# Cross-channel attention on one core: ten of sixteen batches turned by VectorE instead of eight, and the plain copies of G asked for by ScalarE

## The chip, the cores and the metric

One NeuronCore of a Trainium2 chip runs the kernel; nothing else is on the chip. The metric is the device time of one execution in microseconds, smaller is better. Profiles are taken of one execution by the hardware profiler.

## The reference, cut to what matters

X and G (`x`, `ctx`) are 16 batches of 128 x 1024 f32. With rgb = X^T and geo = G^T per batch, 8 heads of 16 channels:

```
attn(q, k) = softmax(q^T k / 4)   per head, 16 x 16, summed over the 1024 positions
rgb_att = rgb + (v_geo attn(q_rgb, k_geo)) proj_p2r^T
geo_att = geo + (v_rgb attn(q_geo, k_rgb)) proj_r2p^T
out     = rgb_att^T + geo_att^T
```

The kernel folds it: one 128 x 128 Gram matrix per batch (X times G^T over the 1024 positions) gives both score matrices after small products with the weights; the softmaxed scores and the weights give two 128 x 128 matrices T, and out = T0 X + T1 G (the identity for the residual is added into T).

## The kernel before, in words

**The work of a batch.** The Gram product needs X and G with positions on the partitions, so both have to be turned. For batches "on tensor" TensorE turns them: 16 transposes of 128 x 128 (line 262), whose PSUM results ScalarE (X, line 402) and VectorE (G, line 478) copy to `xt` and `gt`. For batches "on vector" (`VECTOR_PAIRS`, line 26) the DMA does the coarse part: a pair of batches is loaded a second time in blocks of 1 KB rows into `xz` and `gz` (`load_turned`, line 149), one DMA of 256 KB for each quad, which is a quarter of the 128 partitions (quad 0 is partitions 0 to 31), eight DMAs for a pair's X and G. VectorE's 32 x 32 block transpose (line 471) finishes it, in halves, two of X and two of G per batch. `xz` and `gz` hold two pairs (PAIRS). Every batch is also loaded plainly (X and G, 512 KB each, `x_raw`, `g_raw`, six slots), since the last product needs it unturned: ScalarE rounds it to a high part (`split_hi`, line 389), GpSimd subtracts for the low part (lines 200, 203), and TensorE makes the output in twelve matmuls of 512 columns (line 303). ScalarE copies the output out of PSUM (line 396) and SyncE stores it (line 215, five slots).

**The order.** Every engine runs a hand-written software pipeline over the iteration number i. In iteration i TensorE does, in this order: the output product of batch i-4, the small uv product of i-2, the transposes of batch i if it is on tensor, the y product of i-3, the Gram product of i-1 in two halves, the t product of i-3 and the scores of i-2. VectorE in iteration i turns batch i if it is on vector: first half of X, then the softmax's reciprocal and probabilities of i-3, then first half of G and second half of X, then the copy of y, then the second half of G. ScalarE in iteration i makes the exponentials, splits X of i-2, evacuates the output of i-4, copies uv, splits G of i-2, and copies t.

**Who asks for what.** SyncE asks for all plain copies except batch 0's G: batches 1 to 4 at the start, batch b from 5 on in iteration b-1 if b is on vector and b-3 if not, after waiting until GpSimd is done with batch b-6 in that slot (lines 230 to 234). It asks for quads 0 and 1 of each turned pair (lines 235 to 241) and for the stores, store i-5 in iteration i, which waits for ScalarE's copy. ScalarE asks for quads 2 (early in its iteration) and 3 (after it has split G). Iterations for the turned loads come from `issued_in`: pair 0 in 2, pair 1 in 4, a later pair one iteration after the second batch of the pair two before it; X in that iteration, G in the next.

Of the kernel before, what the change touches and what calls it, by code (L numbers as in the profile page):

```python
# [15 lines left out]
RAW_SLOTS = 6  # L16
# [6 lines left out]
WQR, WKR, WKP, WQP, PP, PR, WVP, WVR = range(8)  # L23


VECTOR_PAIRS = ((5, 6), (8, 9), (11, 12), (14, 15))


def bass_cross_channel_attention(nc: bass.Bass, x, ctx, weights, out):
# [9 lines left out]
    B, C, N = x.shape  # L39
# [5 lines left out]
    on_vector = [b for pair in VECTOR_PAIRS for b in pair]  # L45
# [3 lines left out]
    with ExitStack() as stack:  # L49
# [13 lines left out]
        x_raw = sb("x_raw", [P, RAW_SLOTS, N])  # L63
        g_raw = sb("g_raw", [P, RAW_SLOTS, N])
# [42 lines left out]
        x_loaded = [sem(f"x_loaded{s}") for s in range(RAW_SLOTS)]  # L107
        g_loaded = [sem(f"g_loaded{s}") for s in range(RAW_SLOTS)]
# [32 lines left out]
        x_lo_ready = sem("x_lo_ready")  # L141
        g_lo_ready = sem("g_lo_ready")
# [19 lines left out]
        def x_turned_half(eng, b, half):  # L162
# [3 lines left out]
            else:  # L166
                eng.wait_ge(xt_copied, 2 * on_tensor.index(b) + 1 + half)


        issued_in = {2 + 2 * pair if pair < PAIRS else VECTOR_PAIRS[pair - PAIRS][1] + 1: pair  # L170
                     for pair in range(len(VECTOR_PAIRS))}

# [32 lines left out]

        @block.sync
        def _(sp):
            def load_plain(b):
                slot = b % RAW_SLOTS
                sp.dma_start(x_raw[:, slot, :], x[b]).then_inc(x_loaded[slot], 16)  # L210
                sp.dma_start(g_raw[:, slot, :], ctx[b]).then_inc(g_loaded[slot], 16)

            def store(b):
                sp.wait_ge(half_copied, 2 * b + 2)
                sp.dma_start(out[b], out_sb[:, b % OUT_SLOTS, :]).then_inc(out_stored[b % OUT_SLOTS], 16)

            sp.dma_start(x_raw[:, 0, first], x[0][:, first]).then_inc(x_first, 16)
            sp.dma_start(x_raw[:, 0, second], x[0][:, second]).then_inc(x_loaded[0], 16)
            load_plain(1)
            sp.dma_start(w_sb[:, WQR:WKR + 1, :], weights[:, WQR:WKR + 1, :]).then_inc(wu_loaded, 16)  # L220
            load_plain(2)
            sp.dma_start(w_sb[:, WKP:, :], weights[:, WKP:, :]).then_inc(w_loaded, 16)
            load_plain(3)
            load_plain(4)

            for i in range(2, B + 4):
                for b in range(5, B):
                    if i == max(2, b - 1 if b in on_vector else b - 3):  # L230
                        if b >= RAW_SLOTS:
                            sp.wait_ge(x_lo_ready, b - RAW_SLOTS + 1)
                            sp.wait_ge(g_lo_ready, b - RAW_SLOTS + 1)
                        load_plain(b)
                x_pair, g_pair = issued_in.get(i), issued_in.get(i - 1)
                if x_pair is not None:
                    if x_pair >= PAIRS:
                        pair_turned(sp, x_pair - PAIRS)
                    load_turned(sp, x_turn, xz, xz_loaded, x_pair, (0, 1))
                if g_pair is not None:  # L240
                    load_turned(sp, g_turn, gz, gz_loaded, g_pair, (0, 1))
                if i >= 5:
                    store(i - 5)
            for half in range(2):
                sp.wait_ge(half_copied, 2 * B - 1 + half)
                cols = slice(half * HALF, (half + 1) * HALF)
                sp.dma_start(out[B - 1][:, cols], out_sb[:, (B - 1) % OUT_SLOTS, cols]).then_inc(last_stored[half], 16)
            for s in range(OUT_SLOTS):
                sp.wait_ge(out_stored[s], 16 * len(range(s, B - 1, OUT_SLOTS)))
            for half in range(2):  # L250
                sp.wait_ge(last_stored[half], 16)
# [128 lines left out]
        @block.scalar  # L380
        def _(act):
            def split_hi(b, raw, loaded, hi, hi_ready):
                plain_loaded(act, b, loaded)
                if b == 0:
                    act.wait_ge(x_first, 16)
                    act.wait_ge(g_first, 16)
                if b >= SPLIT_SLOTS:
                    act.wait_ge(half_done, 2 * (b - SPLIT_SLOTS) + 2)
                nc.scalar.copy(hi[:, b % SPLIT_SLOTS, :], raw[:, b % RAW_SLOTS, :]).then_inc(hi_ready, 1)  # L389

            def evacuate(b, half):
                act.wait_ge(half_done, 2 * b + 1 + half)
                if half == 0 and b >= OUT_SLOTS:
                    act.wait_ge(out_stored[b % OUT_SLOTS], 16 * (b // OUT_SLOTS))
                cols = slice(half * HALF, (half + 1) * HALF)
                nc.scalar.copy(out_sb[:, b % OUT_SLOTS, cols], out_ps[:, cols]).then_inc(half_copied, 1)  # L396

            def copy_xt(b, half):
                act.wait_ge(xt_done, 2 * on_tensor.index(b) + 1 + half)
                if b >= 2:  # L400
                    act.wait_ge(gram_done, b - 1)
                nc.scalar.copy(xt[:, b % 2, half * HALF:(half + 1) * HALF], xt_ps[:, :]).then_inc(xt_copied, 1)  # L402

            nc.scalar.dma_start(g_raw[:, 0, first], ctx[0][:, first]).then_inc(g_first, 16)
            nc.scalar.dma_start(g_raw[:, 0, second], ctx[0][:, second]).then_inc(g_loaded[0], 16)

            for i in range(B + 4):
                s, y, l = i - 2, i - 3, i - 4
                x_pair, g_pair = issued_in.get(i), issued_in.get(i - 1)
                if 0 <= s < B:  # L410
                    act.wait_ge(gram_done, s + 1)
                    if s >= 1:
                        act.wait_ge(uv_done, s)
                    nc.scalar.copy(gram_hi[:, :], gram_ps).then_inc(gram_hi_ready, 1)
                if 0 <= y < B:
                    if y >= 1:
                        act.wait_ge(probs_ready, y)
                    for a in range(2):
                        act.wait_ge(s_masked, 2 * y + 1 + a)
                        nc.scalar.activation(expd[:, a, :], scores[:, a, :], ACT.Exp,  # L420
                                             bias=min_neg[:, a:a + 1], scale=-1.0,
                                             accum_out=row_sum[:, a:a + 1]).then_inc(exp_done, 1)
                if 0 <= s < B:
                    split_hi(s, x_raw, x_loaded, x_hi, x_hi_ready)
                if x_pair is not None:
                    if x_pair >= PAIRS:
                        pair_turned(act, x_pair - PAIRS)
                    load_turned(act, x_turn, xz, xz_loaded, x_pair, (2,))
                if g_pair is not None:
                    load_turned(act, g_turn, gz, gz_loaded, g_pair, (2,))  # L430
                if l >= 0:
                    evacuate(l, 0)
                if l >= 0 and l not in (B - 3, B - 2):
                    evacuate(l, 1)
                if 0 <= s < B:
                    act.wait_ge(uv_done, s + 1)
                    if s >= 1:
                        act.wait_ge(s_done, s)
                    nc.scalar.copy(uv[:, :, :], uv_ps.rearrange("p (a c) -> p a c", a=2)).then_inc(uv_copied, 1)
                if i in on_tensor:  # L440
                    copy_xt(i, 0)
                if 0 <= s < B:
                    split_hi(s, g_raw, g_loaded, g_hi, g_hi_ready)
                if x_pair is not None:
                    load_turned(act, x_turn, xz, xz_loaded, x_pair, (3,))
                if g_pair is not None:
                    load_turned(act, g_turn, gz, gz_loaded, g_pair, (3,))
                if i in on_tensor:
                    copy_xt(i, 1)
                if 0 <= y < B:  # L450
                    act.wait_ge(t_summed, y + 1)
                    if y >= 2:
                        act.wait_ge(half_done, 2 * y - 2)
                    nc.scalar.copy(t_hi[:, y % 2, :, :], t_ps.rearrange("p (a c) -> p a c", a=2)).then_inc(t_hi_ready, 1)  # L454
                if l in (B - 3, B - 2):
                    evacuate(l, 1)
                if i == 1:
                    act.wait_ge(wu_loaded, 16)
                    nc.scalar.copy(wu_hi[:, :, :], w_sb[:, WQR:WKR + 1, :]).then_inc(wu_hi_ready, 1)
# [103 lines left out]
```

## Time and profile before

| | us |
|---|---|
| Median of 3 runs (lowest, highest) | 130.85 (130.83, 130.98) |
| The profiled execution | 130.88 |
| Its span, first to last instruction | 128.8 |
| Busy: TensorE / ScalarE / GpSimd / VectorE | 121.5 / 86.3 / 77.3 / 71.2 |

The span is 2.1 us less than the execution's own time; what lies around it is not in the profile. An engine's busy time is the sum over its instructions, so that the distance to the span is time in which it did nothing. A DMA's time to landing runs from its issue until its semaphore is complete, and includes the time in which it stood behind other DMAs of its queue. The DMA share counts packets in flight and can be a little over 1. The 34.25 MB that the profile counts include the weights.

### The profile page before, as it was taken

To read this page: it belongs to the slowest core of one execution; us is meant where nothing else is said; L and a number is where in the kernel's file an instruction comes from. 1 tells how busy PE (TensorE), PEld (TensorE's weight loads), DVE (VectorE), ACT (ScalarE), POOL (GpSimd) and SP (SyncE) were. 2 spreads that over 40 slices of the span, in tenths; PEclk is the share of its full clock that TensorE was granted. 3 is DMA by queue.
4 is the path that set the end of the run, shared out by engine and by line. 5 is a ranking of instruction groups with operands and counts; after the bars stand their busy time and mean duration, and the time that the engine had idled before them with its cause. 6 is when DMAs were issued, how large, how long until landed. Compare 5 with 4: busy or idle time off the path is not lost.

```text
span 128.8 us, 2675 instructions
## 1 busy us (share of the span) xinstructions
PE 121.5 (94%) x858; PEld 109.8 (85%) x858; DVE 71.2 (55%) x210; ACT 86.3 (67%) x194; POOL 77.3 (60%) x41
## 2 busy tenths in 40 slices
PE   6979999999999999999999999999999999979890
PEld 6859998899999999898989898989989898956560
DVE  0045364537878535969633978762787873433410
ACT  3133967875959595768687686779495959595131
POOL 5000779685586877295958386857649595958000
PEclk9999999999999999999999999999999999999998
DMA  3999999999999999999999999999999240400344
GB/s 102 358 416 408 410 312 258 248 248 270 296 211 275 252 384 353 327 242 350 310 270 397 332 325 245 325 304 283 416 416 380 85 163 0 163 0 23 148 165 163
DMA packets 16349, 34.25 MB, mean 266 GB/s; under 512 B 1360, under 2 KB 9680, under 8 KB 16336
## 3 DMA queue, kind: packets, MB, share of 16 engines
q1 hardware_dynamic: 11696, 29.36, 70.9%
q10 hardware_dynamic: 4640, 4.72, 14.2%
q8 instruction: 7, 0.11, 0.4%
q14 instruction: 6, 0.05, 0.1%
HBM read 25.69 MB, written 8.39 MB: 265 GB/s over the span
## 4 chain that ended last, share of the span: by engine, by line
PE 83%; DMA 5%; ACT 4%; issue 2%; DVE 2%; SPq 1%; ACTq 1%
PE out_ps L303 32%; PE gram_bank L283 21%; PE sy_bank L323 6%; DMA g_raw<-in_ctx_dram 5%; PE gt_ps L262 5%; PE xt_ps L262 4%; PE t_bank L359 3%; PE sy_bank L373 3%; PE t_bank L360 3%; PE sy_bank L372 3%; ACT expd L420 2%; PE uv_bank L314 1%; PE uv_bank L316 1%; PE uv_bank L315 1%; DVE probs L512 1%
## 5 line engine op out<-in xcount | busy, mean ns | idle before, releaser
L200 POOL TENSOR_TENSOR x_lo<-x_raw,x_hi 128x1024 fp32r<-128x1024 f32 x16 | 38.0, 2377 | 38.5 <-ACT x_hi L389 38.5
L203 POOL TENSOR_TENSOR g_lo<-g_raw,g_hi 128x1024 fp32r<-128x1024 f32 x16 | 38.0, 2376 | 2.0 <-ACT g_hi L389 2.0
L283 PE MATMUL gram_bank<-gt,xt 128*128 128x128 f32 x256 | 33.8, 275 | 0.0
L283 PEld LDWEIGHTS gram_bank<-gt,xt 128*128 128x128 f32 x256 | 31.2, 192 | 0.0
L396 ACT COPY out_sb<-out_ps 128x512 f32<-128x512 f32 x32 | 18.6, 581 | 4.5 <-PE out_ps L303 3.1
L478 DVE COPY gt<-gt_ps 128x512 f32<-128x512 f32 x16 | 11.0, 688 | 19.1 <-PE gt_ps L262 19.1
L420 ACT ACTIVATE expd<-scores,min_neg 128x128 f32<-128x128 f32 x32 | 12.6, 395 | 8.6 <-DVE min_neg L491 8.6
L389 ACT CAST g_hi<-g_raw 128x1024 fp32r<-128x1024 f32 x16 | 16.9, 1055 | 0.0
L389 ACT CAST x_hi<-x_raw 128x1024 fp32r<-128x1024 f32 x16 | 16.6, 1035 | 0.0
L402 ACT COPY xt<-xt_ps 128x512 f32<-128x512 f32 x16 | 9.4, 587 | 9.2 <-PE xt_ps L262 9.2
L454 ACT CAST t_hi<-t_bank 128x256 fp32r<-128x256 f32 x16 | 6.0, 372 | 14.1 <-DVE t_bank L529 14.1
L303 PE MATMUL out_ps<-x_hi,t_hi 128*128 128x512 f32 x32 | 14.1, 442 | 0.2 <-ACT t_hi L454 0.2
L303 PE MATMUL out_ps<-g_lo,t_hi 128*128 128x512 f32 x32 | 12.8, 399 | 0.0
L303 PE MATMUL out_ps<-x_lo,t_hi 128*128 128x512 f32 x32 | 12.7, 397 | 0.0
L303 PE MATMUL out_ps<-g_hi,t_lo 128*128 128x512 f32 x32 | 12.6, 395 | 0.0
L303 PE MATMUL out_ps<-g_hi,t_hi 128*128 128x512 f32 x32 | 12.6, 395 | 0.0
L303 PE MATMUL out_ps<-x_hi,t_lo 128*128 128x512 f32 x32 | 12.6, 394 | 0.0
L529 DVE TENSOR_TENSOR t_bank<-t_bank,ident 128x256 f32<-128x256 f32 x16 | 6.9, 433 | 9.8 <-PE t_bank L360 9.8
L524 DVE COPY y_sb<-sy_bank 128x256 f32<-128x256 f32 x16 | 6.8, 425 | 9.9 <-PE sy_bank L323 9.9
L471 DVE STREAM_TRANSPOSE gt<-gz 128x512 f32<-128x512 f32 x16 | 11.2, 702 | 0.0
L323 PE MATMUL sy_bank<-w_sb,probs 128*128 128x128 f32 x64 | 9.9, 277 | 1.2 <-DVE probs L512 1.2
L471 DVE STREAM_TRANSPOSE xt<-xz 128x512 f32<-128x512 f32 x16 | 11.0, 685 | 0.0
(49 smaller groups left out, 206.4 us busy)
## 6 DMA issues: line engine op xcount, KB each, us to landing
x_raw<-in_x_dram SPq DMA_DIRECT2D x15, 512.0 KB, 15.1
g_raw<-in_ctx_dram SPq DMA_DIRECT2D x15, 512.0 KB, 14.6
out_dram<-out_sb SPq DMA_DIRECT2D x15, 512.0 KB, 14.5
xz<-in_x_dram SPq DMA_DIRECT2D x8, 256.0 KB, 12.1
gz<-in_ctx_dram SPq DMA_DIRECT2D x8, 256.0 KB, 14.6
xz<-in_x_dram ACTq DMA_DIRECT2D x8, 256.0 KB, 10.8
gz<-in_ctx_dram ACTq DMA_DIRECT2D x8, 256.0 KB, 13.4
x_raw<-in_x_dram SPq DMA_DIRECT2D x2, 256.0 KB, 4.4
```

Of the source, the lines that this page charges most:

```text
L200: nc.gpsimd.tensor_tensor(x_lo[:, slot, :], x_raw[:, raw_slot, :], x_hi[:, slot, :].bitcast(F32), ALU.subtract).then_inc(x_lo_ready, 1)
L203: nc.gpsimd.tensor_tensor(g_lo[:, slot, :], g_raw[:, raw_slot, :], g_hi[:, slot, :].bitcast(F32), ALU.subtract).then_inc(g_lo_ready, 1)
L262: last = nc.tensor.transpose(ps[:, t * TILE:(t + 1) * TILE], raw[:, b % RAW_SLOTS, cols], ident2[:, 0, :])
L283: last = nc.tensor.matmul(gram_ps, xt[:, b % 2, cols], gt[:, b % 2, cols], start=(t == 0), stop=(t == TILES - 1))
L303: last = nc.tensor.matmul(out_ps[:, cols], w[:, b % 2, which, :], moving[:, slot, cols], start=(n == 0), stop=(n == len(parts) - 1))
L323: last = nc.tensor.matmul(y_ps[:, a * P:(a + 1) * P], probs[:, a, :], w_sb[:, wv, :], start=True, stop=True)
L389: nc.scalar.copy(hi[:, b % SPLIT_SLOTS, :], raw[:, b % RAW_SLOTS, :]).then_inc(hi_ready, 1)
L396: nc.scalar.copy(out_sb[:, b % OUT_SLOTS, cols], out_ps[:, cols]).then_inc(half_copied, 1)
L402: nc.scalar.copy(xt[:, b % 2, half * HALF:(half + 1) * HALF], xt_ps[:, :]).then_inc(xt_copied, 1)
L420: nc.scalar.activation(expd[:, a, :], scores[:, a, :], ACT.Exp, bias=min_neg[:, a:a + 1], scale=-1.0, accum_out=row_sum[:, a:a + 1]).then_ ...
L471: nc.vector.transpose(dst[:, b % 2, cols].rearrange("p (j a k) -> p j a k", a=QUADS, k=QUAD), blocks[:, first:first + TILES // 2, :, :]).t ...
L478: nc.vector.tensor_copy(gt[:, b % 2, half * HALF:(half + 1) * HALF], gt_ps[:, :]).then_inc(gt_ready, 1)
```

## The change

`VECTOR_PAIRS` gets a fifth pair and different members: batches 5 to 8 and 10 to 15 are turned by VectorE; TensorE turns 0 to 4 and 9. So 2.10 MB more are loaded (X and G of two batches in turned blocks), and by the rule of `issued_in` pair 1 is asked for in iterations 4 and 5 (X, G) and used from 7, pair 2 in 7 and 8 and used from 10, pair 3 in 9 and 10 and used from 12, pair 4 in 12 and 13 and used from 14. Before, pair 1 was asked for in 4 and 5 and used from 8, pair 2 in 7 and 8 and used from 11, pair 3 in 10 and 11 and used from 14. G's plain copies of batches 1 to 15 are asked for by ScalarE, behind its split of G in the iteration, with the wait for GpSimd's low part of G of batch b-6; SyncE keeps X's with the wait for the low part of X alone. The quads stay divided as they were.

```diff
--- before.py
+++ after.py
@@ -23,7 +23,7 @@
 WQR, WKR, WKP, WQP, PP, PR, WVP, WVR = range(8)
 
 
-VECTOR_PAIRS = ((5, 6), (8, 9), (11, 12), (14, 15))
+VECTOR_PAIRS = ((5, 6), (7, 8), (10, 11), (12, 13), (14, 15))
 
 
 def bass_cross_channel_attention(nc: bass.Bass, x, ctx, weights, out):
@@ -166,6 +166,11 @@
             else:
                 eng.wait_ge(xt_copied, 2 * on_tensor.index(b) + 1 + half)
 
+        def plain_issued_in(i):
+
+
+            return [b for b in range(5, B) if i == max(2, b - 1 if b in on_vector else b - 3)]
+
 
         issued_in = {2 + 2 * pair if pair < PAIRS else VECTOR_PAIRS[pair - PAIRS][1] + 1: pair
                      for pair in range(len(VECTOR_PAIRS))}
@@ -205,10 +210,10 @@
 
         @block.sync
         def _(sp):
-            def load_plain(b):
-                slot = b % RAW_SLOTS
-                sp.dma_start(x_raw[:, slot, :], x[b]).then_inc(x_loaded[slot], 16)
-                sp.dma_start(g_raw[:, slot, :], ctx[b]).then_inc(g_loaded[slot], 16)
+            def load_plain_x(b):
+                if b >= RAW_SLOTS:
+                    sp.wait_ge(x_lo_ready, b - RAW_SLOTS + 1)
+                sp.dma_start(x_raw[:, b % RAW_SLOTS, :], x[b]).then_inc(x_loaded[b % RAW_SLOTS], 16)
 
             def store(b):
                 sp.wait_ge(half_copied, 2 * b + 2)
@@ -216,22 +221,16 @@
 
             sp.dma_start(x_raw[:, 0, first], x[0][:, first]).then_inc(x_first, 16)
             sp.dma_start(x_raw[:, 0, second], x[0][:, second]).then_inc(x_loaded[0], 16)
-            load_plain(1)
+            load_plain_x(1)
             sp.dma_start(w_sb[:, WQR:WKR + 1, :], weights[:, WQR:WKR + 1, :]).then_inc(wu_loaded, 16)
-            load_plain(2)
+            load_plain_x(2)
             sp.dma_start(w_sb[:, WKP:, :], weights[:, WKP:, :]).then_inc(w_loaded, 16)
-            load_plain(3)
-            load_plain(4)
-
-
+            load_plain_x(3)
+            load_plain_x(4)
 
             for i in range(2, B + 4):
-                for b in range(5, B):
-                    if i == max(2, b - 1 if b in on_vector else b - 3):
-                        if b >= RAW_SLOTS:
-                            sp.wait_ge(x_lo_ready, b - RAW_SLOTS + 1)
-                            sp.wait_ge(g_lo_ready, b - RAW_SLOTS + 1)
-                        load_plain(b)
+                for b in plain_issued_in(i):
+                    load_plain_x(b)
                 x_pair, g_pair = issued_in.get(i), issued_in.get(i - 1)
                 if x_pair is not None:
                     if x_pair >= PAIRS:
@@ -388,6 +387,11 @@
                     act.wait_ge(half_done, 2 * (b - SPLIT_SLOTS) + 2)
                 nc.scalar.copy(hi[:, b % SPLIT_SLOTS, :], raw[:, b % RAW_SLOTS, :]).then_inc(hi_ready, 1)
 
+            def load_plain_g(b):
+                if b >= RAW_SLOTS:
+                    act.wait_ge(g_lo_ready, b - RAW_SLOTS + 1)
+                nc.scalar.dma_start(g_raw[:, b % RAW_SLOTS, :], ctx[b]).then_inc(g_loaded[b % RAW_SLOTS], 16)
+
             def evacuate(b, half):
                 act.wait_ge(half_done, 2 * b + 1 + half)
                 if half == 0 and b >= OUT_SLOTS:
@@ -403,6 +407,8 @@
 
             nc.scalar.dma_start(g_raw[:, 0, first], ctx[0][:, first]).then_inc(g_first, 16)
             nc.scalar.dma_start(g_raw[:, 0, second], ctx[0][:, second]).then_inc(g_loaded[0], 16)
+            for b in range(1, 5):
+                load_plain_g(b)
 
             for i in range(B + 4):
                 s, y, l = i - 2, i - 3, i - 4
@@ -441,6 +447,8 @@
                     copy_xt(i, 0)
                 if 0 <= s < B:
                     split_hi(s, g_raw, g_loaded, g_hi, g_hi_ready)
+                for b in plain_issued_in(i):
+                    load_plain_g(b)
                 if x_pair is not None:
                     load_turned(act, x_turn, xz, xz_loaded, x_pair, (3,))
                 if g_pair is not None:
```

## Rows read from the trace of the kernel before

**Rows 1.** The page: busy time by engine, DMA in 40 slices, the chain by engine.
```profile
PE 121.5 (94%) x858; PEld 109.8 (85%) x858; DVE 71.2 (55%) x210; ACT 86.3 (67%) x194; POOL 77.3 (60%) x41
...
DMA  3999999999999999999999999999999240400344
...
PE 83%; DMA 5%; ACT 4%; issue 2%; DVE 2%; SPq 1%; ACTq 1%
```

**Rows 2.** The chain of waits: start us, us, what; where iterations 10, 11, 12, 14 begin.
```profile
64.24 2.81 PE out_ps L303 x12
67.40 0.44 PE xt_ps L262 x4
...
72.28 2.81 PE out_ps L303 x12
...
78.56 2.81 PE out_ps L303 x12
...
92.87 2.80 PE out_ps L303 x12
```

**Rows 3.** Groups by line: the copies of VectorE and ScalarE, and the two turns.
```profile
L478 DVE COPY gt<-gt_ps 128x512 f32<-128x512 f32 x16 | 11.0, 688 | 19.1 <-PE gt_ps L262 19.1
L402 ACT COPY xt<-xt_ps 128x512 f32<-128x512 f32 x16 | 9.4, 587 | 9.2 <-PE xt_ps L262 9.2
L471 DVE STREAM_TRANSPOSE gt<-gz 128x512 f32<-128x512 f32 x16 | 11.2, 702 | 0.0
L471 DVE STREAM_TRANSPOSE xt<-xz 128x512 f32<-128x512 f32 x16 | 11.0, 685 | 0.0
```

**Rows 4.** GpSimd in order of time: the low part of G, batch 10, in iteration 12.
```profile
83.29 2.37 POOL L203 TENSOR_TENSOR g_lo<-g_raw,g_hi 128x1024 fp32r<-128x1024 f32 x1
```

**Rows 5.** The page, DMA queues: packets, MB, share of 16 engines; q1 is SyncE, q10 ScalarE.
```profile
q1 hardware_dynamic: 11696, 29.36, 70.9%
q10 hardware_dynamic: 4640, 4.72, 14.2%
```

**Rows 6.** Busy time by stretch; the last two columns are DMA share and GB/s.
```profile
4.00:96.00 92.00, 90.71 (x661) 83.28 (x659) 56.66 (x162) 65.54 (x148) 57.36 (x25) 1.00 1.06 319
16.00:91.30 75.30, 75.08 (x540) 69.30 (x539) 48.05 (x142) 56.29 (x129) 53.33 (x24) 1.00 1.06 298
92.00:96.00 4.00, 4.00 (x25) 3.46 (x25) 3.97 (x12) 3.23 (x9) 1.17 (x2) 1.00 1.02 418
...
0.00:91.30 91.30, 89.03 (x658) 82.14 (x659) 52.37 (x150) 63.59 (x140) 57.24 (x33) 1.00 1.03 305
...
16.00:20.00 4.00, 3.95 (x34) 3.59 (x32) 2.49 (x10) 2.84 (x9) 3.08 (x3) 1.00 1.04 319
20.00:22.00 2.00, 1.83 (x17) 1.83 (x18) 0.67 (x2) 1.55 (x3) 2.00 (x2) 1.00 1.13 241
```

**Rows 7.** Line 154, G's last quad of pair 3 from ScalarE: start, time to landing.
```profile
L154 ACTq DMA_DIRECT2D gz<-in_ctx_dram x1: 341/341/341, 75.5 to 75.5; - x1
DMA to landing us min/median/max: 15.8/15.8/15.8
```

**Rows 8.** Line 154, G's eight quads from ScalarE together.
```profile
L154 ACTq DMA_DIRECT2D gz<-in_ctx_dram x8: 317/318/341, 17.8 to 75.5; - x8
DMA to landing us min/median/max: 9.2/13.4/15.8
```

**Rows 9.** VectorE in iteration 14: pair 3, first half of G; the copy of y.
```profile
94.76 0.70 DVE L471 STREAM_TRANSPOSE gt<-gz 128x512 f32<-128x512 f32 x1
...
96.50 0.42 DVE L524 COPY y_sb<-sy_bank 128x256 f32<-128x256 f32 x1 [0.45 <-PE sy_bank L323]
```

**Rows 10.** Line 210, batch 14's plain copy of X: start, time to landing.
```profile
L210 SPq DMA_DIRECT2D x_raw<-in_x_dram x1: 1732/1732/1732, 79.9 to 79.9; - x1
DMA to landing us min/median/max: 15.1/15.1/15.1
```

**Rows 11.** After the last matmul; PEclk is the third column from last.
```profile
126.00:128.80 2.80, 0.00 (x0) 0.00 (x0) 0.00 (x0) 0.33 (x1) 0.00 (x0) 0.83 0.43 161
```

## The prediction

> **What bounds the kernel now.** I read the page first: TensorE is busy 94% of the span and makes 83% of the chain that ended last [rows 1]. The DMA line of the same page stands at 9 from the second slice to the thirtieth: until about 97 us the DMA engines are as full as TensorE is [rows 1]. Two resources are at their limit together, and the change takes work from one and gives work to the other. The chain of waits gives the pace of TensorE: iteration 10, whose batch it turns itself, lasts 72.28 - 64.24 = 8.04 us, iteration 11, whose batch VectorE turns, 78.56 - 72.28 = 6.28 us [rows 2]. The difference, 1.76 us, is four groups of four transposes of 0.44 us each, two of X and two of G; one is shown [rows 2].
>
> Then I read how far ahead the data is. G's last quad of pair 3, which ScalarE asked for at 75.54, took 15.8 us and landed at 91.3 [rows 7]. VectorE used it at 94.76 [rows 9]. So a load that was asked for three iterations ahead is there 3.4 us early, no more. The eight quads of G from ScalarE took 9.2 to 15.8 us, 13.4 in the middle [rows 8]; that is queueing, since each is 0.26 MB.
>
> **The change part by part.** *TensorE* loses the 32 transposes of two batches: 2 x 1.76 = 3.52 us, all on the chain [rows 2]. This is the whole gain: 130.88 - 3.52 = 127.4.
>
> *VectorE and ScalarE.* Per batch that moves, VectorE gives two copies of 0.688 and takes two turns of 0.702 and two of 0.685, +1.40 us, and ScalarE gives two copies of 0.587 [rows 3]. VectorE is busy 55% of the span and ScalarE 67% [rows 1], and batches in `VECTOR_PAIRS` already run this program at 6.28 us. Cost nothing; with the cover gone VectorE's would be 2.8 us.
>
> *The asks.* ScalarE gets 15 plain copies and four quads, at 0.32 us each in its queue [rows 8]: 6 us over the kernel, 11 of the plain ones inside the loop at one or two an iteration, where it idles a third of the time; nothing. SyncE gives 15 and gets four; it has time. *The moved wait.* ScalarE now waits for GpSimd's low part of G of batch b-6, and behind that wait stand quad 3, its second copy of X out of PSUM and the copy of t, for which TensorE waits. Tightest is batch 9, asked for in iteration 6 against batch 3, whose low part is made in iteration 5. In iteration 12 that part ends at 83.29 + 2.37 = 85.66, 7.1 us after the iteration began [rows 2, 4]; ScalarE gets to its ask 3.3 us into the next iteration (75.54 - 72.28 [rows 2, 7]), that is 6.28 + 3.3 = 9.6 us after it, 2.5 us later. Cost nothing while TensorE keeps its pace.
>
> *The DMA work.* 2.10 MB more, all in turned blocks. Their price: from 4 to 96 us the DMA engines were full and moved 319 GB/s x 92 us = 29.3 MB [rows 6]. The stretch from 92 to 96 us has plain rows alone and runs at 418 GB/s [rows 6]. The four turned pairs are 8.39 MB, so that the other 21.0 MB would take 50 us at that rate, and 42 us are left for the turned ones: 5.0 us per MB, **10.5 us per pair**. Bounds: at 418 GB/s, 5.0 us; at the mean of the stretch with turned loads in it, 298 GB/s [rows 6], 7.0 us. Two vector batches then need six plain transfers (3.15 MB, 7.5 us) and one pair, 18.0 us of DMA, against 2 x 6.28 = 12.6 us of TensorE. Before, a tensor batch stood between the pairs: 21.8 us of DMA against 20.6 of TensorE, nearly even, as the full DMA line says. After it, pairs follow each other without one in three places of four.
>
> A row shows that full engines can move little: from 20 to 22 us, when the first turned pair is being loaded, the share is 1.13 and only 241 GB/s move [rows 6]. The Trainium skill (SBUF — State Buffer, section "Door 1: The DMA port swizzle") gives a reason: partitions 0 to 63 reach only 8 of the 16 ports, and it gives 218 GB/s for them; by it alone a pair takes 9.6 us. It also says (DMA: Bandwidth & Descriptors, section "Issuing engines are not separate DMA queues") that asking from two engines saves only the time of asking, which speaks against any gain from the moved asks; no run here has shown it yet.
>
> **When pair 4 lands.** In the kernel before, 305 GB/s x 91.3 us = 27.8 MB had moved when G's last quad of pair 3 landed [rows 6]. X of batch 14 was then still on its way (79.86 + 15.1 = 95.0 us [rows 10]). In the changed kernel G of pair 4, the one used from batch 14, is asked for after all of that and more: one more pair (2.10 MB), X and G of batch 14 (1.05), and about a store and a half that was still queued (0.8), 3.95 MB. At 418 GB/s that is 9.4 us, at 298 GB/s 13.3 us, with the turned price of 10.5 us and the rest at 418 it is 14.9 us. I take 14.1, between the last two, since the added part has more turned bytes in it (53%) than that stretch had (37%). Landing: 91.3 + 14.1 = 105.4 us.
>
> It is wanted 3.52 us earlier than before, at 94.76 - 3.52 = 91.2 us, and about 0.5 us of lateness is free (copy of y at 96.50 waits for TensorE by 0.45 us [rows 9]). So **TensorE stands still for 13.7 us in all**, split over pairs 2, 3 and 4, little at pair 2, most at 3 and 4. Net: 13.7 - 3.5 = +10.2 us. Sum: 130.88 + 10.2 = **141.0 us**. From there to the end all is as before. The profiled execution (130.88) lies 0.03 above the median of the runs (130.85), which changes nothing.
>
> *The clock.* After the last matmul, with TensorE idle, the granted clock averages 0.83, that is it fell from its level of 2.4 GHz towards 1.2 GHz within 2.8 us [rows 11]. A standstill of 5 to 7 us could do the same, and the matmuls after it run slower. Price between 0 and 2 us; I take 0, since a slower TensorE before the last standstill is hidden in it, and keep 2 for the range.
>
> **Rivals.** *B, the data comes in time; faster: 127.4.* Pair 4 must then be there by 91.7: 27.8 + 3.95 = 31.8 MB in 91.7 us, 347 GB/s in place of 305. For it: with the plain copies on both queues the two might be full together more often, and from 16 to 20 us, with both queues in turned blocks, 319 GB/s moved [rows 6]; q1 carried 29.4 MB and q10 only 4.7 [rows 5]. Against it: the engines were already full, whatever queue fed them, and 347 is above every stretch with turned blocks that I read. Below 347 GB/s the gain shrinks by 0.26 us per GB/s, and at about 333 GB/s the change comes out even.
>
> *C, only the last pair is late, because it is asked for late.* ScalarE asks for G's last quad 3.3 us into iteration 13 and VectorE wants it 1.9 us into iteration 14 [rows 2, 9]: 6.28 - 3.3 + 1.9 + 0.5 = 5.4 us for a load that took 9.2 to 15.8 [rows 8]. This costs 3.8 to 10.4 us however well the DMA runs: 127.4 + 3.8 to 10.4 = 131.2 to 137.8. It is the floor under the forecast too, unless the queues run empty. The condition is that the mean rate is good enough for pairs 2 and 3 (about 335 GB/s).
>
> *D, ScalarE is held in its own asks.* If its DMA queue fills, the ask itself lasts longer, and everything behind it on ScalarE with it; that comes on top: 143 to 147. The case that the change does not do what it says is small: the transposes are gone for certain; the asks that are moved may bring nothing, and the sum counts nothing for them.
>
> **How the numbers follow.** Forecast 0.70 (own range 136 to 144.5), B 0.12 (127.4 to 130.6), C 0.12, D 0.06. Faster by over 0.2%, about what a measurement can tell from no change here: 0.11, all from B; within 0.2%: 0.03, between B and C; slower 0.86. The range leaves out most of B and the upper end of D: 132.5 to 145.5.
>
> **What the profile after would show.** Line 262 with 96 transposes in place of 128, VectorE's turns of X and of G 20 each. DMA moved 36.3 MB and the line of nines reaches about 110 us. In the chain, DMA `gz` stands with some 10 us, and VectorE waits at line 471 in iterations 12 and 14, TensorE after it. G's last quad of pair 4 lands near 105. Wrong would be: no idle of VectorE before its turns of G; a rate above 340 GB/s up to 90 us; ScalarE's asks longer than 0.4 us (then D).

## The result, and the profile after

The changed kernel takes 139.9 us (median of four runs, 138.8 to 141.6) against 130.9, a ratio of 1.066 (95% interval 1.059 to 1.073). It is slower by 9.0 us; 141.0 was forecast. The profiled execution took 139.08 us with a span of 136.9, 8.1 us longer than the span before. Medians and ranges here are over all executions of a kernel, and ratios only over those within 1.5% of its fastest; where that is a single one, no ratio is stated.

The page of the changed kernel: busy time by engine, three of the lines in 40 slices, the two DMA queues, the chain by engine, three of the DMA issues (the last number is the median time to landing).

```profile
PE 121.7 (89%) x826; PEld 109.3 (80%) x826; DVE 73.9 (54%) x214; ACT 84.1 (61%) x190; POOL 77.4 (57%) x41
...
PE   7958999999999999999999999996509999979790
PEclk9999999999999999999999999999755799999999
DMA  4999999999999999999999999999994030300434
...
q1 hardware_dynamic: 10624, 22.55, 51.3%
q10 hardware_dynamic: 7888, 13.63, 32.0%
...
PE 59%; DMA 26%; ACT 4%; issue 3%; DVE 3%; SPq 1%; ACTq 1%; DVEq 0%
...
x_raw<-in_x_dram SPq DMA_DIRECT2D x15, 512.0 KB, 16.4
g_raw<-in_ctx_dram ACTq DMA_DIRECT2D x15, 512.0 KB, 9.5
gz<-in_ctx_dram ACTq DMA_DIRECT2D x10, 256.0 KB, 11.6
```

TensorE is as busy as before in microseconds and less in share: 121.7 us in a longer span [rows 1]. It has 32 transposes (3.5 us) less to do, but part of its work now runs at the lower clock (below). The slices show where it stopped: one gap in the digits 6, 5 and 0, about 92 to 103 us, with the granted clock low in it and behind it. The DMA line is full up to there, without a gap. In the chain the DMA has gone from 5% to 26%. ScalarE's queue now moves 13.6 MB, SyncE's 22.6 [rows 5].

The chain of waits of the changed kernel (start us, us, what). Each `out_ps` row is the beginning of an iteration: 4, 5, 8, 9, 10, 13, 15, 16.

```profile
2.59 10.96 DMA x_raw<-in_x_dram
...
24.35 2.79 PE out_ps L302 x12
...
32.38 2.82 PE out_ps L302 x12
...
51.80 2.81 PE out_ps L302 x12
...
58.08 2.81 PE out_ps L302 x12
...
66.11 2.80 PE out_ps L302 x12
...
85.04 2.82 PE out_ps L302 x12
...
88.70 12.62 DMA gz<-in_ctx_dram
...
103.00 0.80 PE t_bank L358 x2
103.80 0.43 PE t_bank L359 x2
104.23 1.71 PE gram_bank L282 x8
...
106.79 3.27 PE out_ps L302 x12
...
111.74 0.22 PE t_bank L358 x2
...
113.53 2.81 PE out_ps L302 x12
```

Four things are to be seen. Iteration 4 begins at 24.35; before, it began at 23.05 (`23.05 2.81 PE out_ps L303 x12` in the chain of the kernel before), and a wait for X's plain copy now stands at the head of the chain. Iterations 5 to 7 last 19.42 us in place of 3 x 6.28 = 18.84. Iterations 10 to 12 run at pace: from 66.11 to 85.04 are 18.93 us, 0.1 too long. Iterations 13 and 14 last from 85.04 to 106.79, 21.75 us in place of 12.56: here 9.2 us are lost. The sum is -3.5 + 1.3 + 0.6 + 0.1 + 9.2, and 0.5 in the output product that begins at 106.79 (3.27 in place of 2.81): +8.2 us, which is the difference of the spans.

VectorE in order of time, its turns that waited for a load (in brackets the idle time before, and what ended it):

```profile
48.08 0.71 DVE L479 STREAM_TRANSPOSE gt<-gz 128x512 f32<-128x512 f32 x1 [1.17 <-DMA gz<-in_ctx_dram]
...
81.32 0.71 DVE L479 STREAM_TRANSPOSE gt<-gz 128x512 f32<-128x512 f32 x1 [0.68 <-DMA gz<-in_ctx_dram]
...
94.78 0.71 DVE L479 STREAM_TRANSPOSE xt<-xz 128x512 f32<-128x512 f32 x1 [2.71 <-DMA xz<-in_x_dram]
...
101.34 0.71 DVE L479 STREAM_TRANSPOSE gt<-gz 128x512 f32<-128x512 f32 x1 [4.97 <-DMA gz<-in_ctx_dram]
```

Pair 1 is late by 1.2 us in iteration 7 and pair 3 by 0.7 in iteration 12, where TensorE loses the 0.1 us. In iteration 14 VectorE waits 2.7 us for the last quad of X and then 5.0 for the last of G. No turn of pair 2 waited.

Busy time by stretch (TensorE's clock and the GB/s are the third from last and the last column):

```profile
0.00:101.30 101.30, 92.83 (x665) 84.73 (x665) 58.39 (x165) 66.09 (x147) 63.23 (x35) 0.98 1.04 322
16.00:91.30 75.30, 74.71 (x530) 68.73 (x531) 51.92 (x149) 55.97 (x128) 54.30 (x24) 1.00 1.07 319
101.00:106.00 5.00, 3.00 (x14) 3.00 (x15) 3.08 (x6) 0.40 (x2) 0.00 (x0) 0.50 0.59 240
108.00:110.00 2.00, 2.00 (x10) 1.61 (x9) 1.94 (x5) 1.52 (x4) 0.82 (x1) 1.00 0.00 0
```

While G's last quad was on its way, 322 GB/s x 101.3 us = 32.6 MB had moved. From 16 to 91.3 us the engines moved 319 GB/s, where the kernel before moved 298 with as full a share [rows 6]. And from 101 to 106 us, at the end of the standstill and after it, the clock is granted at 0.50, the 1.2 GHz level; from 108 us on it is back at 1.00.

### The profile page after: what moved, and what is told of

It reads as the page before. It is cut to its first block, busy times and chain, and to the rows that moved or that the text cites. A ratio compares the mean times of both kernels' runs of the same rounds, so it can differ in the third digit from the quotient of the medians.

```text
span 136.9 us, 2603 instructions
## 1 busy us (share of the span) xinstructions
PE 121.7 (89%) x826; PEld 109.3 (80%) x826; DVE 73.9 (54%) x214; ACT 84.1 (61%) x190; POOL 77.4 (57%) x41
## 4 chain that ended last, share of the span: by engine, by line
PE 59%; DMA 26%; ACT 4%; issue 3%; DVE 3%; SPq 1%; ACTq 1%; DVEq 0%
PE out_ps L302 25%; DMA gz<-in_ctx_dram 18%; PE gram_bank L282 14%; DMA x_raw<-in_x_dram 8%; PE sy_bank L322 4%; PE t_bank L358 3%; PE xt_ps L261 3%; PE sy_bank L372 2%; PE t_bank L359 2%; PE sy_bank L371 2%; PE gt_ps L261 2%; ACT expd L426 2%; DVE xt L479 1%; DVE y_sb L532 1%; PE uv_bank L313 1%
## 5 line engine op out<-in xcount | busy, mean ns | idle before, releaser
L282 PE MATMUL gram_bank<-gt,xt 128*128 128x128 f32 x256 | 35.1, 282 | 0.0
L282 PEld LDWEIGHTS gram_bank<-gt,xt 128*128 128x128 f32 x256 | 32.4, 198 | 0.0
L426 ACT ACTIVATE expd<-scores,min_neg 128x128 f32<-128x128 f32 x32 | 12.6, 395 | 9.0 <-DVE min_neg L499 9.0
L479 DVE STREAM_TRANSPOSE gt<-gz 128x512 f32<-128x512 f32 x20 | 14.1, 702 | 6.8 <-DMA gz<-in_ctx_dram 6.8
L486 DVE COPY gt<-gt_ps 128x512 f32<-128x512 f32 x12 | 8.3, 688 | 16.2 <-PE gt_ps L261 16.2
L479 DVE STREAM_TRANSPOSE xt<-xz 128x512 f32<-128x512 f32 x20 | 13.7, 686 | 2.7 <-DMA xz<-in_x_dram 2.7
L302 PE MATMUL out_ps<-g_hi,t_lo 128*128 128x512 f32 x32 | 12.6, 395 | 0.0
L302 PE MATMUL out_ps<-x_hi,t_lo 128*128 128x512 f32 x32 | 12.6, 394 | 0.0
L358 PE MATMUL t_bank<-w_sb,y_sb 128*128 128x128 f32 x32 | 7.0, 301 | 5.3 <-DVE y_sb L532 5.3
L322 PEld LDWEIGHTS sy_bank<-w_sb,probs 128*128 128x128 f32 x64 | 8.4, 190 | 4.0 <-issue 4.0
```

The lines of the kernel that those rows point to most:

```text
L282: last = nc.tensor.matmul(gram_ps, xt[:, b % 2, cols], gt[:, b % 2, cols], start=(t == 0), stop=(t == TILES - 1))
L302: last = nc.tensor.matmul(out_ps[:, cols], w[:, b % 2, which, :], moving[:, slot, cols], start=(n == 0), stop=(n == len(parts) - 1))
L322: last = nc.tensor.matmul(y_ps[:, a * P:(a + 1) * P], probs[:, a, :], w_sb[:, wv, :], start=True, stop=True)
L358: nc.tensor.matmul(t_ps[:, 0:P], y_sb[:, 1, :], w_sb[:, PR, :], start=True, stop=True)
L479: nc.vector.transpose(dst[:, b % 2, cols].rearrange("p (j a k) -> p j a k", a=QUADS, k=QUAD), blocks[:, first:first + TILES // 2, :, :]).t ...
L486: nc.vector.tensor_copy(gt[:, b % 2, half * HALF:(half + 1) * HALF], gt_ps[:, :]).then_inc(gt_ready, 1)
```

## The experiments

Two theories were put against each other. S: the DMA engines cannot move the bytes in time, wherever the asks stand. A: the last pair is late because it is asked for late, two iterations before its use, into a queue that is 9 to 18 us long.

**Each half of the change alone.** The first run takes the kernel before and only its table of pairs:

```diff
-VECTOR_PAIRS = ((5, 6), (8, 9), (11, 12), (14, 15))
+VECTOR_PAIRS = ((5, 6), (7, 8), (10, 11), (12, 13), (14, 15))
```

> The kernel before with the five pairs of the change, all plain copies still asked for by SyncE. Theory A (the last pair is late because it is asked for late, two iterations before its use, and its queue is 9 to 13 us long): G's last quad is asked for at the same place, so the standstill of some 7 us in iteration 14 stays and the time is 137 to 140 us. Theory S (the DMA engines cannot deliver; what the forecast held): pairs 2 and 3 are late too, the rate between 16 and 91 us stays near 298 GB/s, and the time is 140 to 143 us. If the moved asks raise the rate (319 GB/s in the changed kernel), this run is slower than the changed kernel; if they do nothing it is equal, less the 1.3 us by which the changed kernel starts later.

The second takes the changed kernel with the four pairs of before:

```diff
-VECTOR_PAIRS = ((5, 6), (7, 8), (10, 11), (12, 13), (14, 15))
+VECTOR_PAIRS = ((5, 6), (8, 9), (11, 12), (14, 15))
```

> The changed kernel with the four pairs of before: the moved asks alone. Both theories: no standstill in the loop, since the pairs are asked for three iterations ahead. The start is 1.3 us later as in the changed kernel, because X of batch 2 lands at 13.6 in place of 10.7 us, so 131.5 to 132.5 us. If the moved asks raise the DMA rate, the line of nines ends before 97 us and pair 3 lands earlier than 91.3 us.

The pairs alone: 140.5 us (136.0 to 142.2). The asks alone: 132.0 us (131.6 to 132.3), ratio 1.008 (1.006 to 1.011). VectorE of the first, all its turns that waited:

```profile
79.53 0.71 DVE L471 STREAM_TRANSPOSE gt<-gz 128x512 f32<-128x512 f32 x1 [0.91 <-DMA gz<-in_ctx_dram]
...
92.88 0.71 DVE L471 STREAM_TRANSPOSE xt<-xz 128x512 f32<-128x512 f32 x1 [2.60 <-DMA xz<-in_x_dram]
...
101.36 0.71 DVE L471 STREAM_TRANSPOSE gt<-gz 128x512 f32<-128x512 f32 x1 [6.78 <-DMA gz<-in_ctx_dram]
```

The chain of waits of the second, its head and iteration 4:

```profile
2.58 10.83 DMA x_raw<-in_x_dram
...
24.21 2.81 PE out_ps L302 x12
```

Busy time by stretch of the second:

```profile
16.00:91.30 75.30, 75.07 (x538) 69.30 (x539) 47.71 (x141) 56.79 (x129) 52.77 (x24) 1.00 1.06 315
```

The pairs make the loss, and at the same place: G's last quad is used at 101.36, in the changed kernel at 101.34. The time does not part the theories here (140.5 lies at the edge of both), the place does: pair 2 never waits and pair 3 only 0.9 us, where theory S had both late. The moved asks alone cost 1.0 us; iteration 4 begins at 24.21, 1.2 us late.

Whether the moved asks raise the rate is open. With five pairs, 316 GB/s moved from 16 to 91.3 us without them and 319 with them. With four pairs it was 298 without them (the kernel before [rows 6]) and 315 with them, though pair 3 landed no earlier for it: its last quad of G was asked for at 77.1 and took 14.6 us, to 91.7, against 91.3. The Trainium skill says (DMA: Bandwidth & Descriptors, section "Issuing engines are not separate DMA queues") that asking from several engines saves only the time of asking. The two kernels with five pairs agree with that, the two with four do not; each rate is from one execution.

**The ask of the last pair, and the bytes before it.** In the changed kernel, ScalarE's four quads of pair 4 together, early in iteration 12:

```diff
-                    load_turned(act, x_turn, xz, xz_loaded, x_pair, (2,))
-                if g_pair is not None:
+                    load_turned(act, x_turn, xz, xz_loaded, x_pair, (2, 3) if x_pair == LAST else (2,))
+                    if x_pair == LAST:
+                        load_turned(act, g_turn, gz, gz_loaded, x_pair, (2, 3))
+                if g_pair is not None and g_pair != LAST:
...
-                if x_pair is not None:
+                if x_pair is not None and x_pair != LAST:
                     load_turned(act, x_turn, xz, xz_loaded, x_pair, (3,))
-                if g_pair is not None:
+                if g_pair is not None and g_pair != LAST:
                     load_turned(act, g_turn, gz, gz_loaded, g_pair, (3,))
```

> The changed kernel, but ScalarE asks for its four quads of pair 4 (X and G, quads 2 and 3) together early in iteration 12, as soon as the buffers are free, in place of over iterations 12 and 13. Theory A: G's last quad is asked for 9 us earlier and lands 4 to 6 us earlier (its queue is still some 12 us long and the four quads follow one another), at 95 to 97 us; the standstill shrinks to 3 to 5 us: 133 to 136 us. Theory S (bytes alone): it only overtakes the plain copies of G of batches 13 and 14, 1.05 MB or 2.5 to 3 us: 136 to 137 us.

(`LAST` is 4, the last pair.) And in the changed kernel, less to move with the asks where they were. The second halves of the plain copies of batches 10 to 15 are not loaded, so part of the outputs of these batches is not computed from their inputs. The same edit is made for G on ScalarE's side:

```diff
-                sp.dma_start(x_raw[:, b % RAW_SLOTS, :], x[b]).then_inc(x_loaded[b % RAW_SLOTS], 16)
+                n = HALF if b >= 10 else N
+                sp.dma_start(x_raw[:, b % RAW_SLOTS, 0:n], x[b][:, 0:n]).then_inc(x_loaded[b % RAW_SLOTS], 16)
```

> The changed kernel with the plain copies of batches 10 to 15 loading only the first 512 of 1024 columns (the second halves of those slots keep older data, so that part of the outputs of these batches is not computed from its inputs). Asks stand where they stood; 2.6 MB less are ahead of pair 4. Theory S: pair 4 lands 6 to 8 us earlier and the standstill nearly goes: 129.5 to 132 us. Theory A (a late ask alone): an ask at 88.7 us is wanted at 93.8; even in shorter queues a quad needs 8.4 us or more, so 3 to 4 us of standstill stay: 132 to 135 us.

The early ask: 133.0 us (132.5 to 134.9), ratio 1.015 (1.011 to 1.019). The lighter load: 133.4 us (131.1 to 134.6). The profiled execution of the early ask was its slowest (134.9), that of the lighter load its fastest (131.1). VectorE of the early ask:

```profile
49.16 0.71 DVE L482 STREAM_TRANSPOSE gt<-gz 128x512 f32<-128x512 f32 x1 [2.47 <-DMA gz<-in_ctx_dram]
...
83.01 0.71 DVE L482 STREAM_TRANSPOSE gt<-gz 128x512 f32<-128x512 f32 x1 [1.29 <-DMA gz<-in_ctx_dram]
...
97.89 0.71 DVE L482 STREAM_TRANSPOSE gt<-gz 128x512 f32<-128x512 f32 x1 [2.90 <-DMA gz<-in_ctx_dram]
```

VectorE of the lighter load:

```profile
92.26 0.71 DVE L481 STREAM_TRANSPOSE xt<-xz 128x512 f32<-128x512 f32 x1 [0.78 <-DMA xz<-in_x_dram]
...
95.69 0.71 DVE L481 STREAM_TRANSPOSE gt<-gz 128x512 f32<-128x512 f32 x1 [2.21 <-DMA gz<-in_ctx_dram]
```

The last quad of G in the chain of waits (when it was asked for, and how long it took), in the early ask and in the lighter load:

```profile
82.06 15.80 DMA gz<-in_ctx_dram
...
88.11 7.55 DMA gz<-in_ctx_dram
```

In the changed kernel it was asked for at 88.70 and took 12.62. The early ask, 6.6 us earlier, brings the landing forward by 3.5 us; three waits of 2.5, 1.3 and 2.9 us are left. With less to move the ask stands where it stood and takes 5.1 us less, and 0.8 + 2.2 us of waits are left in iteration 14 (the 8.4 us that the expectation put under every quad did not hold). So both the place of the ask and the bytes before it decide when the quad lands.

The early ask moves no byte less and takes back 6.9 us of the 9.0 by the medians, where theory S allowed 2.5 to 3. Not all of this is the landing: the clock, which both theories left out, fell less (0.987 over the profiled execution in place of 0.963, and 1.00 in two of the four runs), and the landing itself moved by little more than theory S allowed. So this run speaks against S in its pure form and does not settle it. Nor does the lighter load: its 133.4 us lies in theory A's range (132 to 135) and above S's (129.5 to 132), but its fastest execution in S's. The runs with a third buffer settle it.

**The same early ask, with SyncE asking for all plain copies** (the edit of the early ask, made to the pairs-alone kernel):

> The five pairs, two buffers, plain copies asked for by SyncE as before, and ScalarE asks for its four quads of pair 4 together early in iteration 12. Against the run with the early ask and the moved plain copies (132.5 to 133.4 us) it shows what the moved asks are worth: both theories say the later start of 1.3 us goes away, 131 to 132.5 us. If the moved asks help the last pair (ScalarE's own queue is shorter for its quads here, so they need not), it is slower than 133 us.

It missed: 138.1 us (137.0 to 141.9), ratio 1.051 (1.043 to 1.059), slower than with the moved asks where 131 to 132.5 was expected. Line 155 (`load_turned`) of this kernel, G's two quads of pair 4 from SyncE, then from ScalarE (shortest, middle and longest time of the ask itself in ns, first and last start, and time to landing); then SyncE's ask that stood before its two.

```profile
L155 SPq DMA_DIRECT2D gz<-in_ctx_dram x2: 1537/1850/2164, 83.7 to 85.3; - x2
DMA to landing us min/median/max: 15.3/15.9/16.6
...
L155 ACTq DMA_DIRECT2D gz<-in_ctx_dram x2: 515/516/516, 78.2 to 78.8; - x2
DMA to landing us min/median/max: 14.0/14.7/15.4
...
78.92 4.78 SPq L212 DMA_DIRECT2D g_raw<-in_ctx_dram  x1
```

The same two quads of SyncE in the early-ask kernel with the moved asks:

```profile
L155 SPq DMA_DIRECT2D gz<-in_ctx_dram x2: 432/480/529, 80.1 to 80.5; - x2
DMA to landing us min/median/max: 12.9/13.1/13.3
```

ScalarE's quads are there by 78.8 + 15.4 = 94.2. Now SyncE's are last: it reaches them at 83.7 and 85.3, since the ask before them, G's plain copy of batch 14, alone held it for 4.8 us; they land at 101.9. With the moved asks they are asked for at 80.1 and 80.5 and are there by 93.8. So the moved asks do have a worth here, of some 5 us, which both theories had missed; it is hidden in the change itself, where ScalarE's last quad is later than either. (The two runs were made on two chips, on both of which the kernel before measures 131.0, so the size is not certain.)

**A third buffer for the turned pairs**, so that pair 4 need not wait until pair 2 is turned. First with SyncE asking for all plain copies:

```diff
-PAIRS = 2
+PAIRS = 3
...
-        issued_in = {2 + 2 * pair if pair < PAIRS else VECTOR_PAIRS[pair - PAIRS][1] + 1: pair
-                     for pair in range(len(VECTOR_PAIRS))}
+        issued_in = {2: 0, 4: 1, 7: 2, 9: 3, 10: 4}
```

> The five pairs with the plain copies asked for by SyncE as before, and a third buffer for the turned pairs, so that pair 4 is asked for in iterations 10 (X) and 11 (G) in place of 12 and 13; nothing else moves. Theory A (late ask of the last pair): pair 4 lands before iteration 14, no standstill there, and the 3.5 us of transposes come through but for what pairs 1 and 3 and the plain copies behind it lose: 127.5 to 130 us. Theory S (bytes): the same bytes are due by the same time, and what is gained at pair 4 is lost at pair 3 or at the plain copies of batches 12 to 14 that it has overtaken: 133 us or more.

With `11: 4` in place of `10: 4`:

> As the run with the third buffer, but pair 4 is asked for in iterations 11 and 12. Theory A: the ask of G's last quad stands at 5.4 + 6.3 = 11.7 us before its use, and the queue is 9 to 15 us long, so 0 to 3 us of standstill are left: 128.5 to 132 us. Theory S: as with iterations 10 and 11, 133 us or more.

138.5 us (134.2 to 142.3) and 133.0 us (131.9 to 137.2; ratio 1.011, 1.007 to 1.016). The profiled execution of the first can't be set beside the others, since it ran with a lower clock throughout (below). The second, 132.95 us, lies between the two theories (A 128.5 to 132, S 133 or more). So the same was tried in the changed kernel with its own asks; then with the start as before; then with pair 4 in 11; and the start alone with two buffers. The edit of the start, of which one of four added lines is shown; G of batches 2, 3 and 4 likewise stands behind X of its batch:

```diff
             load_plain_x(1)
+            sp.dma_start(g_raw[:, 1, :], ctx[1]).then_inc(g_loaded[1], 16)
...
-            for b in range(1, 5):
-                load_plain_g(b)
```

> The changed kernel with its own asks, and the third buffer for the turned pairs, pair 4 asked for in iterations 10 and 11. Theory A (each ask too late for a queue of 9 to 18 us, whichever queue it is): all quads of pair 4 land before iteration 14, no standstill, and only the later start of 1.3 us is left against 127.4: 128.5 to 130 us. Theory S (bytes): 132 us or more, with the standstill moved to pair 3 or to the plain copies.

> As the run before it, with the plain copies of G of batches 1 to 4 asked for by SyncE in the order of the kernel before. X of batch 2 then lands near 10.7 in place of 13.6 us and the start is not late: theory A 127.3 to 129 us. Theory S: 1.3 us less than the run before it, still above 131 us.

> As the run before it, with pair 4 asked for in iterations 11 and 12: theory A leaves 0 to 2 us of standstill at pair 4 and takes less from pair 3: 127.5 to 131 us; theory S as there.

> The changed kernel with two buffers, and only the start as in the kernel before (SyncE asks for G of batches 1 to 4). If the late start is due to these asks, iteration 4 begins at 23.0 in place of 24.3 us. The standstill at pair 4 is set by the asks in iterations 12 and 13, which move with TensorE: the time falls by 0.5 to 1.5 us to 137.5 to 139.5. If the bytes set the landing of pair 4, the start does not matter and the time stays at that of the changed kernel.

| third buffer | start as before | pair 4 asked for in | us (range) | ratio (interval) |
|---|---|---|---|---|
| yes | no | 10, 11 | 136.4 (135.0 to 139.6) | 1.034 (1.030 to 1.038) |
| yes | yes | 10, 11 | 135.0 (134.0 to 135.7) | 1.030 (1.025 to 1.036) |
| yes | yes | 11, 12 | 129.8 (128.5 to 132.0) | 0.988 (0.983 to 0.994) |
| no | yes | 12, 13 | 139.4 (136.9 to 142.3) | not stated |

VectorE with pair 4 in 10 and 11, start as before; this is pair 3, in iteration 12:

```profile
85.02 0.71 DVE L480 STREAM_TRANSPOSE gt<-gz 128x512 f32<-128x512 f32 x1 [5.83 <-DMA gz<-in_ctx_dram]
```

VectorE with pair 4 in 11 and 12:

```profile
47.60 0.71 DVE L480 STREAM_TRANSPOSE gt<-gz 128x512 f32<-128x512 f32 x1 [1.85 <-DMA gz<-in_ctx_dram]
...
93.94 0.71 DVE L480 STREAM_TRANSPOSE gt<-gz 128x512 f32<-128x512 f32 x1 [1.22 <-DMA gz<-in_ctx_dram]
```

With pair 4 asked for two iterations earlier its own turns no longer wait, and pair 3, whose quads of G stand among those of pair 4's X, waits 5.8 us. This is what theory S had said of it, the standstill moved to pair 3, and theory A's 128.5 to 130 and 127.3 to 129 us were wrong (136.4 and 135.0 measured). One iteration earlier is right for both: 1.9 us of wait at pair 1 and 1.2 at pair 4 are left and TensorE's clock stays at its higher level for all of the span. Here theory A's range held and theory S's, above 131 us, did not. The second and third rows of the table move the same bytes on the same chip and differ only in when pair 4 is asked for: 135.0 and 129.8 us. With pair 4 in 12 and 13, the fourth row, it is 139.4. No theory that counts bytes alone gives these three. (The expectation of the last experiment puts the 1.9 us in iteration 14; they are those of pair 1.)

This version is 1.1 us faster than the kernel before (129.8 against 130.9, on the same chip), the only one measured that is; the interval leaves out 1, but one of its four runs, 132.0, was slower than the kernel before. Against the same asks in the kernel with SyncE's plain copies (133.0 us, on another chip) it shows again what the moved asks are worth: there SyncE asked for its last quad of G of pair 4 at 81.6 us and it took 18.0, here at 71.6 and 16.2.

The start alone: iteration 4 began again at 23.0 (the chain of waits of the last row of the table):

```profile
23.04 2.80 PE out_ps L306 x12
```

The time stayed where it was, within 136.9 to 142.3 us, a spread too wide to show the 1.3 us. In the profiled execution, the slowest, pair 3 waited 3.2 us and pair 4 1.7 + 6.0. With the third buffer (first two rows) the earlier start came with 1.5 us less.

**The last quads together in the fastest version:**

```diff
-                    load_turned(act, g_turn, gz, gz_loaded, g_pair, (2,))
+                    load_turned(act, g_turn, gz, gz_loaded, g_pair, (2, 3) if g_pair == 4 else (2,))
```

> The fastest version so far (third buffer, pair 4 asked for in iterations 11 and 12, moved asks, start as before), with ScalarE's two quads of G of pair 4 asked for together early in iteration 12 in place of the second one 3 us later. Theory A: the last of ScalarE's quads lands up to 3 us earlier, the 1.9 us of standstill in iteration 14 shrink to under 1, and the time is 127.5 to 129.5 us. Theory S: two quads in a row only wait for each other and the plain copy of G of batch 13 now stands behind them; no change, 128.5 to 130.1 us.

It missed both: 135.2 us (133.9 to 135.6), ratio 1.026 (1.019 to 1.033). VectorE:

```profile
81.53 0.71 DVE L480 STREAM_TRANSPOSE gt<-gz 128x512 f32<-128x512 f32 x1 [1.91 <-DMA gz<-in_ctx_dram]
...
98.43 0.71 DVE L480 STREAM_TRANSPOSE gt<-gz 128x512 f32<-128x512 f32 x1 [4.94 <-DMA gz<-in_ctx_dram]
```

ScalarE's second quad of G, the one that the edit moves, in the chain of waits:

```profile
78.66 19.75 DMA gz<-in_ctx_dram
```

It is asked for 3.2 us earlier than in the fastest version (81.86), takes 19.8 us in place of 12.1 and lands 4.5 us later; SyncE's two are there by 91.5. So the quad that was to land earlier is the one that is late. But this run was on another chip, and it differs before the edit can act: SyncE asks for its quads of G of pair 4 at 75.6 in place of 71.1 us, and pair 3 waits 1.9 us where the fastest version waited for nothing. On this chip the kernel before, too, took 132.2 to 132.7 us in five of eleven runs, against 130.7 to 131.2 in all its runs on the other chips. What of the 5 us is the edit and what the chip is open, and with it whether the 129.8 us hold on every chip.

## Why the prediction was right

**The gain, 3.52 us, as forecast.** All iterations whose batch VectorE turns last 6.28 us where nothing waits, and the chain shows no other price for VectorE's turns.

**The bytes, as forecast; their pace mis-sized.** 31.8 MB were put ahead of the landing of pair 4, and 32.6 MB had moved by then. The sum let the first 27.8 MB take 91.3 us as before and gave the other 3.95 MB 14.1 us (280 GB/s, from the price of a turned pair). With the same full share the changed kernel had a higher pace all along: 319 GB/s from 16 to 91.3 us in place of 298, 322 up to the landing, which came at 101.3 in place of 105.4. That is 4.1 us too much in the sum.

**The place of the standstill was wrong.** It was spread over pairs 2, 3 and 4, most at 3 and 4. Pair 2 was on time and pair 3 late by 0.7 us. Rival C had the place and the reason, the ask 5.4 us before the use. Its price, 12.6 - 5.4 = 7.2 us with the time to landing that was measured, gives 127.4 + 7.2 = 134.6, and with what no one had counted, 1.3 us at the start, 0.7 at pairs 1 and 3 and 2.5 of clock (below), 139.1 us; the profiled execution took 139.08. C's own range, 131.2 to 137.8, left these three out. The runs put the two together: the early ask and the lighter load each remove most of the loss. The forecast's mechanism (full DMA engines) makes the queue long, and rival C's (the ask two iterations ahead) makes it matter. The pair-3 wait of 5.8 us, when pair 4 overtakes it, shows that neither can be left out.

**The moved asks were not free.** They were costed at nothing. On ScalarE that held inside the loop: its fifteen plain asks took 0.35 us in the middle and 1.04 at most, and no wait of ScalarE for GpSimd shows among the waits. Missed was the start: ScalarE asks for G of batches 1 to 4 at once from 1.7 us on, X of batch 2, which SyncE asks for at 2.6, lands at 13.6 in place of 10.7, and TensorE starts 1.3 us late; the run of the asks alone took 1.0 us more. Missed as well was SyncE's side, "it has time": the price of an ask, 0.32 us, was read from ScalarE alone, while a single ask held SyncE for up to 4.1 us here and 4.8 in the early ask with SyncE's plain copies. Pair 1 cost 0.6 us.

**The clock was taken at nothing, 2 us kept for it.** From 103.00 to 107.5 us the granted clock was 0.50. The work from 103.00 to 110.06 in the chain took 7.06 us; the same work one iteration later took 4.59: 2.5 us. The landing 4.1 us early and these 2.5 us behind it make 141.0 - 4.1 + 2.5 = 139.4, near the 139.08 of the profiled execution. (The late start does not belong in this sum, which counts from the landing: in the kernel with the pairs alone, which starts on time, the same quad is used at 101.36.) That the total came within 1.1 us of the median is in part luck: two sizes were off in opposite directions, and the place was wrong.

**Rival B** wanted 347 GB/s up to 91.7 us; none of the runs with five full pairs had it. The fastest version moved 332 up to 91.3 us, close to the 333 at which B's reckoning came out even, and was 1.1 us faster than the kernel before. **D** did not occur: single asks of ScalarE did take up to 1.4 us, more than the 0.4 that was to be its sign, but asks of ScalarE make 1% of the chain, as before, and the time lies below D's 143 to 147.

## What to carry to other kernels

Where two resources are full together, as here, work taken from one and given to the other is not hidden: look at how early the loads land, and not only at how busy the engines are. With queues of 9 to 18 us, as here, the place of an ask was worth as much as its bytes (133.0 and 133.4 us): ask one more iteration ahead of the last consumer, with a buffer for it, and not so early that it overtakes the load before it. Issues moved between queues change which one is last; check each quad of a load that several engines ask for.

## What the runs showed of the hardware that was not expected

Full DMA engines are not a fixed rate: with the share at 1.06 to 1.07, the kernel before moved 298 GB/s from 16 to 91.3 us and the changed one 319, the kernel with the pairs alone 316 and the fastest version 330. No run tells why. Kernels that wait for the DMA spread wide: the pairs alone took 136 to 142 us in one set of runs, while the kernel before stayed within 130.7 to 131.1 in that set (on the chip of the last experiment it, too, took 130.8 to 132.7).

TensorE idled for 2.0 us ahead of 96.5 and for 4.5 us ahead of 103.0; by 101 the clock was at 1.2 GHz (0.50), and the work from 103.0 to about 107.5 still ran at that level. In one execution (the third buffer with SyncE's plain copies) it was granted at neither level but at 0.85 for the whole loop; the iterations then lasted 6.9 in place of 6.28 us, and nearly no load was late. Busy time of that execution from 20 to 40 us:

```profile
20.00:40.00 20.00, 19.94 (x134) 18.30 (x133) 11.06 (x32) 13.49 (x30) 14.01 (x6) 0.85 1.08 250
```
